# Two-layer transformer block on one core: a slot's extra pieces between its two pairs of products, its PV products last, on all engines

## The reference, cut to what matters

```python
x = L0_attn_x; xn = layernorm(x)
# layer 0: attention over all keys, with rotary embedding, and a top-2-of-8 mixture of experts
Q = rope(xn @ wq.T); K = rope(xn @ wk.T); V = xn @ wv.T
out = softmax(Q K.T / sqrt(8)) V          # per head
x = x + out @ wo.T + wo_b + sum_e combine_w[e] * (relu(xn @ w1[e] + b1[e]) @ w2[e] + b2[e])
xn = layernorm(x)
# layer 1: causal attention, no embedding, and a gated feed-forward in 4-bit blocks of 16
x = x + softmax(causal(q k.T) / sqrt(8)) v @ Wo.T + fp4_linear(silu(fp4_linear(xn, wg)) * fp4_linear(xn, wu), wd)
```

## Time and profile before

| what | us |
|---|---|
| median of 3 runs | 1615.34 (1614.98 to 1619.94) |
| the profiled execution, as a run | 1609.59 |
| its span | 1607.9 |
| TensorE busy | 1459.2 (91%) |
| VectorE busy | 1338.0 (83%) |
| ScalarE busy | 1129.9 (70%) |
| GpSimd busy | 576.2 (36%) |

### The profile page before, as it was taken

How to read it: one execution, slowest core, us unless ns; L and a number is a source line. 1 busy time by engine, 2 the same in 40 slices (tenths; PEclk the granted TensorE clock), 3 DMA queues, 4 the chain that set the end, 5 groups by cost and what they waited for, 6 DMA issues and landing times.

```text
span 1607.9 us, 34216 instructions
## 1 busy us (share of the span) xinstructions
PE 1459.2 (91%) x10557; PEld 582.2 (36%) x10557; DVE 1338.0 (83%) x3450; ACT 1129.9 (70%) x2580; POOL 576.2 (36%) x531
## 2 busy tenths in 40 slices
PE   3978999999999999989999999999999988899986
PEld 1112344443334453433333444333444323323322
DVE  6999877789887888898998778889888878888880
ACT  2167678788788577778878557777878845765675
POOL 3002302103244646424444451230623564543520
PEclk8599999999999999999999889999999988999999
DMA  6303273333362253323511135142742101500000
GB/s 173 100 8 99 65 185 116 105 87 92 95 162 65 76 145 88 89 78 100 125 35 51 48 93 141 52 113 78 185 104 79 34 19 46 114 2 15 2 2 14
DMA packets 169833, 131.84 MB, mean 82 GB/s; under 512 B 31597, under 2 KB 143158, under 8 KB 169654
## 3 DMA queue, kind: packets, MB, share of 16 engines
q1 hardware_dynamic: 165562, 121.26, 28.6%
q0 software_dynamic: 4096, 8.40, 1.8%
HBM read 88.50 MB, written 40.50 MB: 80 GB/s over the span
## 4 chain that ended last, share of the span: by engine, by line
PE 60%; DVE 23%; issue 7%; ACT 5%; POOL 2%; DMA 2%; SPq 1%; DVEq 0%; ACTq 0%; POOLq 0%
PE ring L521 38%; PE pO L521 18%; DVE mparts L1180 13%; PE ring L524 4%; ACT PR L833 3%; DVE junk L1184 2%; DVE xr L1360 1%; DVE stats L1230 1%; DVE xn L1247 1%; ACT hid L904 1%; DVE hs L1468 1%; POOL rstd L731 1%; DVE msplit L1418 1%; DVE hs L1472 0%; ACT parts L527 0%
## 5 line engine op out<-in xcount | busy, mean ns | idle before, releaser
L833 ACT ACTIVATE PR<-ring 128x512 f32<-128x512 f32 (+3 forms) x1792 | 881.9, 557 | 331.4 <-PE ring L521 327.4
L1180 DVE TENSOR_REDUCE mparts<-ring 128x1 f32<-128x512 f32 x1280 | 807.4, 682 | 87.1 <-PE ring L521 78.5
L521 PE MATMUL ring<-QX,KX 50*128 50x512 bf16 (+3 forms) x1792 | 541.6, 367 | 75.6 <-DVE mparts L1180 34.2
L521 PE MATMUL ring<-KX,QX 48*128 48x512 bf16 (+3 forms) x1792 | 555.8, 374 | 14.2 <-DMA QX<-scratch 14.1
L521 PE MATMUL pO<-PR,VX 128*18 128x512 f32 (+3 forms) x3584 | 446.9, 572 | 9.4 <-ACT PR L833 8.2
L521 PEld LDWEIGHTS ring<-QX,KX 50*128 50x128 bf16 x1792 | 126.0, 94 | 606.4 <-ACT PR L833 208.3
L1184 DVE CUSTOM_DVE_ANT_0 junk<-ring,diag 128x384 bf16<-128x384 f32 (+3 forms) x512 | 228.3, 486 | 48.6 <-PE ring L521 45.6
L790 POOL TENSOR_SCALAR bq<-bq 128x352 f32<-128x352 f32 (+1 forms) x40 | 47.1, 1177 | 324.7 <-ACT bq L943 324.5
L763 POOL DMA_INDIRECT rows_in<-xn,at x64 | 62.6, 978 | 257.3 <-PE pO L521 172.1
L521 PEld LDWEIGHTS ring<-KX,QX 48*128 48x128 bf16 x1792 | 125.8, 94 | 33.6 <-DVE mparts L1180 17.9
L904 ACT ACTIVATE hid<-ring,b1r 128x128 f32<-128x128 f32 x368 | 105.1, 370 | 25.0 <-PE ring L521 23.9
(11 more groups left out here) (165 smaller groups left out, 1345.8 us busy)
## 6 DMA issues: line engine op xcount, KB each, us to landing
w1r<-in_w SPq DMA_DIRECT2D x92, 256.0 KB
w2r<-in_w SPq DMA_DIRECT2D x92, 256.0 KB
scratch<-parts SPq DMA_DIRECT2D x48, 256.0 KB, 3.3
scratch<-parts SPq DMA_DIRECT2D x96, 128.0 KB, 2.4
KX<-scratch SPq DMA_DIRECT2D x64, 192.0 KB, 4.4
QX<-scratch SPq DMA_DIRECT2D x128, 96.0 KB, 4.5
xg<-rows_in SPq DMA_DIRECT2D x92, 64.0 KB
rows_out<-yx SPq DMA_DIRECT2D x92, 64.0 KB
```

Source lines behind the costliest of these rows:

```text
L521: return nc.tensor.matmul(dst, lhsT, rhs, start=start, stop=stop, **kw)
L833: nc.scalar.activation(PR[:, n % 2, HALF * j + off:HALF * j + HALF], ring[plan.bank("E", k)][:, off:HALF], ACT.Exp, scale=SCALE).then_inc( ...
L1180: v.tensor_reduce(dst, src[:, 0:w], axis=X, op=ALU.max).then_inc(s_mr, 1)
```

## The change

In every slot the extras move ahead of pair 1, PV moves behind it, and the other engines and the ring's numbering follow. TensorE: pair 0, extras, pair 1, PV. ScalarE: exponentials 0 and 1, `act`, readers of extras, exponentials 2 and 3, `out`, `late`. VectorE: maxima 0 and 1, quarters 0 and 1, readers of extras, maxima 2 and 3, combine, quarters 2 and 3. The planner's slots, SP's and GpSimd's lists are the same. The blocks themselves are moved as they are; the diff is cut to their heads.

```diff
@@ number
-            for j in range(4):
-                for kind, key, n in (("E", s["step"], self.steps), ("M", s["quad"], self.quads)):
-                    if key is not None:
-                        k = 4 * n[key] + j
-                        self.at[kind][k] = len(self.ring)
-                        self.ring.append((kind, k))
+            self.pairs(s, 0)
             for e in s["xs"]:
...
+            self.pairs(s, 1)
+
+    def pairs(self, s, pair):
+        for j in (2 * pair, 2 * pair + 1):
+            for kind, key, n in (("E", s["step"], self.steps), ("M", s["quad"], self.quads)):
+                if key is not None:
+                    k = 4 * n[key] + j
+                    self.at[kind][k] = len(self.ring)
+                    self.ring.append((kind, k))
@@ scalar
                     exps(s, (0, 1))
-                    if s["out"] is not None:
...
-                        copy(oT[k % 2][:, :], pO[:, :]).then_inc(s_oT, 1)
                     for e in s["act"]:
...
-                    exps(s, (2, 3))
                     for e in s["xs"]:
...
+                    exps(s, (2, 3))
+                    if s["out"] is not None:
...
+                        copy(oT[k % 2][:, :], pO[:, :]).then_inc(s_oT, 1)
                     for e in s["late"]:
@@ tensor
                     products(s, 0)
-                    if s["pv"] is not None:
...
-                        ins.then_inc(s_pv, 1)
-                    products(s, 1)
                     for e in s["xs"]:
...
                         ins.then_inc(s_x, 1)
+                    products(s, 1)
+                    if s["pv"] is not None:
...
+                        ins.then_inc(s_pv, 1)
@@ vector
                     for e in s["small"][0] + s["small"][1]:
                         small_step(e)
-                    maxima(s, (2, 3))
-                    if s["combine"] is not None:
...
-                    for e in s["small"][2]:
                         small_step(e)
                     for e in s["xs"]:
...
+                    maxima(s, (2, 3))
+                    if s["combine"] is not None:
...
+                    for e in s["small"][2]:
+                        small_step(e)
                     for e in s["small"][3]:
                         small_step(e)
```

More of the change, by code:

```diff
@@ L929, in _ @@
                                 copy(wdT[0:FL, FC1 - 1, :], src[0:FL, (FC1 - 1) * P:FC1 * P]).then_inc(s_freed["A"], 1)
+                    exps(s, (2, 3))
+                    if s["out"] is not None:
+                        k = plan.outs[s["out"]]
+                        act.wait_ge(s_pv, plan.steps[s["pv"]] + 1)
+                        if k == 0:
+                            act.wait_ge(s_lo, 4)
+                        if k >= 2:
+                            act.wait_ge(s_x, filled(("fin",) + list(plan.outs)[k - 2]))
+                        copy(oT[k % 2][:, :], pO[:, :]).then_inc(s_oT, 1)
                     for e in s["late"]:
@@ L1144, in _ @@
                         ins.then_inc(s_x, 1)
+                    products(s, 1)
+                    if s["pv"] is not None:
+                        p, g, qh, kt = s["pv"]
+                        n = plan.steps[s["pv"]]
+                        last_kt = plan.kts(p, qh) - 1
+                        off = 0 if PHASES[p][0] == 0 else max(0, P * (kt - TH * qh))
+                        if g == 0 and qh == 0 and kt == 0:
+                            for h in range(NH):
+                                pe.wait_ge(*freed(("v", p, h)))
+                        if n == 0:
+                            pe.wait_ge(s_zero, 1)
+                        pe.wait_ge(s_ex, 4 * (n + 1))
+                        first = kt == 0 and g % 2 == 0
+                        if first and plan.outs[p, g // 2, qh]:
+                            pe.wait_ge(s_oT, plan.outs[p, g // 2, qh])
+                        for j in range(G):
+                            h = G * g + j
+                            ins = mm(pO[OW * j:OW * j + 2 * VC, off:HALF], values(p, h, kt),
+                                     PR[:, n % 2, HALF * j + off:HALF * j + HALF],
+                                     start=first, stop=kt == last_kt and g % 2 == 1, skip_group_check=True)
+                        ins.then_inc(s_pv, 1)
             @block.vector
@@ L1485, in _ @@
                             v.tensor_tensor(sums(n), sums(n), left(n), ALU.add).then_inc(s_sum, 1)
+                    maxima(s, (2, 3))
+                    if s["combine"] is not None:
+                        layer = PHASES[s["combine"][0]][0]
+                        dve.wait_ge(s_mr, 4 * (plan.quads[s["quad"]] + 1))
+                        link(v.tensor_reduce(mneg[:, :], mparts[layer][:, s["combine"][2], :, :], axis=X, op=ALU.max,
+                                             negate=True))
+                        link(v.tensor_copy(msplit[:, 0:G * TH], mneg[:, :]))
+                        v.tensor_tensor(msplit[:, G * TH:2 * G * TH], mneg[:, :], msplit[:, 0:G * TH],
+                                        ALU.subtract).then_inc(s_ng, 1)
+                    for e in s["small"][2]:
+                        small_step(e)
                     for e in s["small"][3]:
```

8 lines of the change are left out of this document (removed).

## The result

| | before | after |
|---|---|---|
| median, us | 1616.87 (6 runs) | 1645.19 (6 runs, 1637.97 to 1647.07) |
| ratio after / before | | 1.0157, 95% interval 1.0129 to 1.0185 |
| profiled execution: run, span, us | 1609.59, 1607.9 | 1638.18, 1636.4 |
| TensorE busy, us | 1459.2 | 1460.5 |

The change costs 28 us by the medians (25 by the ratio) where +9 was forecast: the sign was right, the size about three times too small. Ratios compare across chips better than medians do.

The account below looks back on a forecast made before the run. The prediction took TensorE to limit in some stretches and VectorE in others. Its terms, 14 + 4 - 6.5 - 0.5 - 2 = +9 us, added to the median 1615.34 gave 1624 us; range for 8 in 10: 1598 to 1645.

Parts of the forecast that it names:

- Where the limit lies: Whole run: no engine is full; TensorE limits in some stretches (265.78 to 299.76 us), VectorE in others (1399.2 to 1405).
- The shift itself: TensorE queue: the new order is the old one moved by half a slot, same work and distances; costed at nothing.
- Term 1: Combine to transpose of the maxima: TensorE stands 21 us over 64 combines, two thirds counted: +14 us (0 to 38).
- Term 2: Copy of the output accumulator to its transpose: TensorE stands up to 0.33 us, 32 times; +4 us (0 to 10.6).
- Term 3: PV no longer waits for exponentials: -6.5 us (-7.9 to -4) in the last twelve slots, -0.5 us elsewhere.
- Term 4: ScalarE's split parts: GpSimd's sums come half a slot earlier for their reader; -2 us (-10 to 0).
- Term 5: GpSimd's pace and DMA queues: scatters and even gathers go half a slot later; 0 us (-3 to +3).
- A: Rival: waits are covered and more even VectorE lumps help; -13 us, 1602 us; sign VectorE waits under 110 us; chance 0.27.
- B: Rival: no change, combine and copy waits cancel against the gains; 1615 us; chance 0.22.
- C: Rival: combine waits bring more stretches at the lower clock; 1644 us; sign mean clock under 0.94; chance 0.13.

Follow-up runs that it names:

- e9: Kernel before with only the product stream, its exponentials and reductions half a slot ahead, and a second buffer for partial maxima: 1598.76 us, ratio 0.9916.
- e1: Changed kernel with the transpose of the maxima and its reader put back behind pair 1, ahead of PV: 1628.15 us, ratio 1.0099.
- e3: Changed kernel with the transposes of the maxima and of the copied accumulator both put back behind pair 1: 1628.84 us, ratio 1.0098.
- e4: Changed kernel, block order kept, with the transpose of the maxima planned two slots after its combine instead of one: 1626.08 us, ratio 1.0083.
- e5: Changed kernel, block order kept, with every extra that waits for input from outside the extras planned one slot later: 1628.91 us, ratio 1.0105.
- e6: Kernel before with only PV and its copy moved last in the slot (pair 0, pair 1, extras, PV): 1743.33 us, ratio 1.0796.
- e12: e10 with VectorE's small steps and ScalarE's split and late parts half a slot later: 1605.07 us, ratio 0.9941.
- e11: e10 with products, PV, copy and combine planned one slot later, so extras stand on TensorE as in the changed kernel: 1643.59 us, ratio 1.0168.
- e10: e9 with the combine directly behind the slot's last reductions and no second buffer of the maxima: 1602.64 us, ratio 0.9940.
- e2: Changed kernel with the transpose of the copied accumulator and its reader put back behind pair 1: 1643.58 us, ratio 1.0195.
- e7: Kernel before with the new block order only from slot 474 on, the last twelve steps: 1606.10 us, ratio 0.9958.
- e8: New block order below slot 388 only, the old order behind it: 1637.98 us, ratio 1.0148.

## Why the prediction was right in sign and wrong in size

**Where the limit lies.** Right. In the stretch where TensorE had no idle time it now has 0.99 us in 34, and the run got longer by about what TensorE stands more.

**The shift itself.** "I cost that at nothing" holds: e9 makes exactly that shift, at 0.9916. e1, e3, e4 and e5 seemed to speak against it. They give back an edge by other means: e1 and e3 put an extra next to PV, with no pair between, which e6 shows to be costly when the extra is long; e4 and e5 planned the extras anew. In these four TensorE stands 10 to 19 us more than in the kernel before, most of it in front of products (95 to 111 us; 89.8 before). Such a wait alone explains nothing: e12 has 101.8 us of it and is faster than the kernel before. That e1's and e3's rest comes from the neighbourhood of extra and PV is argued, not shown, and the transpose of the maxima is short (0.23 us); nor did I find out why e5, with all edges loose, keeps 1%. This is the open end of the case.

**Term 1, the combine (+14).** This is the step that was mis-sized most. The mechanism, the place and the releaser are as said. The 15 slots with fp were nearly right: 0.6 us each forecast, 0.74 measured (11.0 us). The 49 others were put at 0.25 us each, 12 us in all; they are 0.94 each, 45.9 us. The 2.38 us from the pair's start to the end of the combine came from one place. In the kernel before that is the smallest value that occurs: 21 of the 64 combines take up to 2.45 us, the mean is 3.00, because VectorE often still has reductions, small steps or an extra's result to do when the pair arrives (in the 43 longer ones it is idle for only 0.18 us on average between the pair's start and the combine's end). The earlier trace rows showed such a place, which I used only to argue that a wait costs nothing there. With the mean, the wait comes to 3.00 + 0.15 (handover) - 2.2 = 0.95 us a combine. A hidden share of a third fits the sums: the waits for products fell by 17.6 us where mtr and fin rose by 57.7, 31%. But 10.9 of the 56.9 us stood in front of the transpose before, too, and only 46.0 are new. So the term was 21 x 2/3 = 14 and should have been some 46.0 x 2/3 = 31 us. This figure rests on standing times. The two runs that take just this wait away give back less, 0.6% (e1) and 0.7% (e4), or 9 and 12 us, for the reasons left open above; e11, with both edges, costs 2.3% against e10.

**Term 2, copy and transpose of pO (+4).** The standing was forecast at up to 10.6 us and rose by 11.7, to 13.0 us in 30 places. Giving back this edge alone (e2) gained nothing. The four microseconds can be neither shown nor excluded; e11 shows the two edges together only.

**Term 3, PV behind its exponentials (-6.5 and -0.5).** Right: PV's wait 9.4 to 1.8 us, and e7, which has the new order in the tail alone, is 6.8 us faster by the ratio (3.6 to 10.0 us). Its profile shows the wait of PV gone as well:

```profile
PE pO L529 <- ACT PR L841: 1.8, 3, 1.1
```

**Term 4, split parts (-2).** The waits fell as said, from 19.9 to 3.1 us, and no gain shows: e12 has this placing and e10 hasn't, at the same ratio (0.9941 and 0.9940).

**Term 5, GpSimd and DMA (0).** Nothing speaks against it. The scatters wait 264.9 us for PV instead of 172.1, but e11, with 177.1, is as slow as the changed kernel.

**The rivals.** A (regrouping helps) is out: VectorE waits 146.1 us for products, not under 110. B is out by the interval. C named 1644 us, nearly the measured time, but its mechanism can be at most a part. TensorE's busy time is 1460.5 against 1459.2 us, and its new standing time, 27.1 us, fills the span's growth. A number that fits shows no cause. Yet C isn't out altogether. In the profiled execution of the changed kernel the clock was at the lower level for 181 us, 151 of them with TensorE busy, against 158 and 130 before, and the mean clock of its six runs is 0.939 to 0.945, where C's sign was under 0.94. Half of the 21 us of additional busy time at the lower level, an estimate of 10 us, is the most that the clock can have cost there; the busy time as a whole doesn't show it. That the new gaps bring the lower clock is not shown either. In e6, with 99.8 us more of standing, TensorE is busy 40.2 us more, at a mean clock of 0.935; e11 against e10 was given above. The Trainium skill, "TensorE: Matmul & The Clock Gate", section "A second HAM failure mode: psum-queue depth-cycling", says that short gaps between groups of products can let the clock oscillate; e6 and e11 agree with it in direction, and for the changed kernel it stays open.

With term 1 at 31 instead of 14, the sum of the prediction would have been +26 us; +28 was measured by the medians, +25 by the ratio.

## What to carry to other kernels

Price an edge by all places where it occurs: the one timeline in which everything runs smoothly gives the shortest path of the producer, here 2.38 us against a mean of 3.00. The wait there was 0.40 us (forecast 0.25), where the mean over 64 places was 0.89. Before you reorder the blocks of an in-order queue, list which producer and consumer change places, and look for an equivalent move that keeps all of these pairs apart: moving the product stream ahead of the rest (e9) gave a gain of 0.8%, where the reordering lost 1.6%. And when an experiment gives an edge back, check that it doesn't bring two long blocks together or plan anew, or its remainder may be taken for a cost of the change.

## What the runs showed of the hardware

The clock of the same instructions differs from one execution to the next. In the tail both the kernel before and e8 run the old order; the stretches below (length, busy times of PE, PEld, DVE, ACT and POOL, clock, DMA share, GB/s) are the last of the kernel before and the last of e8:

```profile
1575.00:1607.00 32.00, 18.68 (x160) 6.72 (x156) 1.53 (x4) 16.53 (x40) 0.00 (x0) 0.89 0.06 17
```
```profile
1580.00:1600.00 20.00, 16.33 (x137) 4.30 (x131) 7.88 (x25) 14.37 (x33) 0.00 (x0) 0.95 0.01 2
1600.00:1634.00 34.00, 23.11 (x118) 6.47 (x114) 1.53 (x4) 12.11 (x28) 0.00 (x0) 0.50 0.05 15
```

In e8 the last 34 us ran at 0.50, the lower of the two levels, and its last seven steps took 6.7 us longer. TensorE had been busy 16.33 of 20 us before that, at 0.95. Where the clock doesn't differ, profiles repeat closely: e7, which is the kernel before up to slot 474, keeps its distance to it within 0.5 us from 294 to 1069 us. From 1436 to 1452 us the granted clock was 1.00 in the kernel before and 0.68 in e7, and there e7 falls back by about 4 us with the same code. So a difference of a microsecond between stretches can be read from two single profiles only where their clocks agree; one change of the clock is worth more.
